# Projection and turn of the next heads behind the first value product in every attention group, four feed-forward tiles in TensorE's loop, and the order of SyncE's pad writes

## The reference, cut to what matters

```
kv   = concatenate([xn @ Wkv.T, ln @ Wlkv.T])          # 64 context rows and 1024 normed token rows
q    = ln @ Wq.T
attn = softmax(rmsnorm(q) * SCALE @ rmsnorm(k).T + mask)
x    = x + tanh(g_xattn) * ((attn @ v) @ Wo.T + bo)
probs = softmax(layernorm(x) @ w_router); top 2 of 8 experts per token
x    = x + tanh(g_ffn) * sum over the 2 experts of weight * (gelu(y @ w1 + b1) @ w2 + b2)
```

## Time and profile before

| | |
|---|---|
| median of 3 runs | 915.76 us |
| the profiled execution: own time | 922.48 us |
| its span | 920.7 us |
| TensorE matmuls, busy | 856.9 us, 93% of the span |
| VectorE busy | 647.2 us, 70% |
| ScalarE busy | 514.5 us, 56% |
| GpSimd busy | 331.9 us, 36% |
| mean granted TensorE clock | 0.989 of full speed |

### The profile page before, as it was taken

The page is one execution under the profiler, slowest core; times in us unless marked ns, Lnnn a source line. Parts: engine busy times, 40 slices in busy tenths (PEclk is TensorE's granted clock), DMA queues, the critical chain, the costliest instruction groups (busy, mean ns, idle before and its releaser), DMA issues.

```text
span 920.7 us, 19517 instructions
## 1 busy us (share of the span) xinstructions
PE 856.9 (93%) x5968; PEld 656.6 (71%) x5968; DVE 647.2 (70%) x1500; ACT 514.5 (56%) x1371; POOL 331.9 (36%) x241
## 2 busy tenths in 40 slices
PE   3898899998999989999999998999999999999995
PEld 3644455554455544554459998999999999999995
DVE  5767667677776767667697788775756776676695
ACT  2668676687757878558762654443433443353462
POOL 2332323323285322653134328532322223232233
PEclk9899999999999999999999999999999999999998
DMA  4801000120012201120034449452342525253272
GB/s 126 243 1 49 1 1 1 47 94 1 1 51 88 93 1 47 41 92 18 1 104 122 118 102 255 103 142 46 85 94 46 133 48 139 46 137 49 37 229 24
DMA packets 71899, 70.32 MB, mean 76 GB/s; under 512 B 18592, under 2 KB 66976, under 8 KB 71840
## 3 DMA queue, kind: packets, MB, share of 16 engines
q1 hardware_dynamic: 57696, 52.73, 19.5%
q0 software_dynamic: 13152, 16.86, 10.5%
q10 hardware_dynamic: 992, 0.00, 0.1%
HBM read 44.04 MB, written 26.31 MB: 76 GB/s over the span
## 4 chain that ended last, share of the span: by engine, by line
PE 47%; issue 15%; DVE 15%; POOL 10%; DMA 5%; ACT 5%; SPq 2%; another core or an unknown queue 1%; DVEq 0%; POOLq 0%; ACTq 0%
PE psS L1685 17%; PE psF L1881 8%; PE psO L1881 8%; POOL rr L676 6%; PE psO L1818 4%; DMA lnf<-routed 4%; PE psS L1802 4%; POOL routed L686 4%; DVE p_sum L1136 3%; PE psF L1685 2%; PE psF L1849 1%; ACT sq L823 1%; DMA xr<-in_x 1%; ACT p_ring L867 1%; DVE qkd L1110 1%
## 5 line engine op out<-in xcount | busy, mean ns | idle before, releaser
L884 ACT ACTIVATE V<-psS,b_col 128x256 f32<-128x256 f32 x280 | 117.0, 470 | 212.2 <-PE psS L1685 193.3
L694 POOL DMA_INDIRECT out<-V,token_i x70 | 122.5, 1749 | 262.6 <-DVE V L1327 241.7
L676 POOL TENSOR_TENSOR rr<-ssm,minus_half 128x4 f32<-128x4 f32 (+1 forms) x72 | 119.0, 1652 | 255.1 <-DVE ssm L1100 254.9
L867 ACT ACTIVATE p_ring<-psS,shift 128x1024 f32<-128x1024 f32 x128 | 136.5, 1111 | 70.4 <-PE psS L1802 70.2
L1818 PE MATMUL psO<-p_ring,V 128*64 128x512 f32 x576 | 149.2, 615 | 0.0
L1136 DVE TENSOR_TENSOR p_sum<-p_sum,p_ring 128x1024 f32<-128x1024 f32 (+1 forms) x112 | 136.1, 1215 | 0.8
L1881 PE MATMUL psF<-ln_hi,K 128*128 128x256 f32 x560 | 123.7, 284 | 0.3 <-DVE K L1306 0.3
L1802 PE MATMUL psS<-Q,K 64*128 64x512 f32 x864 | 121.4, 413 | 0.2 <-ACT p_ring L867 0.2
L1802 PEld LDWEIGHTS psS<-Q,K 64*128 64x128 f32 x864 | 77.2, 187 | 61.4 <-issue 43.5
L1881 PE MATMUL psO<-ln_hi,K 128*128 128x256 f32 x560 | 120.5, 279 | 0.0
L1306 DVE TENSOR_TENSOR K<-V,K 128x512 fp32r<-128x512 f32 x140 | 97.1, 693 | 4.8
(11 more groups left out here) (289 smaller groups left out, 1761.1 us busy)
## 6 DMA issues: line engine op xcount, KB each, us to landing
xr<-in_L_ffn_w SPq DMA_DIRECT2D x11, 1024.0 KB, 8.3
xn<-in_L_ffn_w SPq DMA_DIRECT2D x11, 1024.0 KB, 5.4
lnf<-routed SPq DMA_DIRECT2D x35, 258.0 KB
routed<-pad_rows SPq DMA_DIRECT2D x17, 258.0 KB, 9.5
xr<-in_x SPq DMA_DIRECT2D x8, 512.0 KB, 4.5
xb<-in_x SPq DMA_DIRECT2D x4, 1024.0 KB, 5.9
out<-xb SPq DMA_DIRECT2D x4, 1024.0 KB, 4.7
b_raw<-in_L_ffn_b SPq DMA_DIRECT2D x11, 128.0 KB, 3.1
```

The source lines that it names most:

```text
L676: pool.tensor_tensor(rr[0:p, c % 2, n], ssm[0:p, c % 2, n], minus_half[0:p, n], ALU.pow).then_inc(rr_ready, 1)
L694: pool.indirect_dma_start(out_rows, bass.IndirectOffsetOnAxis(ap=token_i[:, m:m + 1], axis=0), y_out[:, m, :], None, bounds_check=NTOK - 1 ...
L867: act.activation(p_ring[0:p, u % RING, :], psS[u % 2][0:p].rearrange("p a n -> p (a n)"), ACT.Exp, bias=bias).then_inc(exp_done, 1)
L884: act.activation(g32[:, q % 2, (c % 2) * TM:(c % 2 + 1) * TM], psH[q][:, (c % 2) * TM:(c % 2 + 1) * TM], ACT.Gelu_apprx_tanh, bias=b1_col[ ...
```

## The change

Four edits. (1) In the attention `tile_steps` stands behind the first value product in all groups. (2) In the last window the ranks of the sequence before move from the late uses of group 5 to behind the scores of group 6, ahead of the sums. (3) On TensorE tiles 5 to 8 of the feed-forward part go into the loop. (4) SyncE writes five of the eight pads before `load_rows(7)` and three behind it.

```diff
@@ mid_uses and late_uses
+                if w + 1 == WINDOWS and i == 6:
+                    return [("ranks", b - 1)]
...
-                    if i == (5 if last else 6):
+                    if i == 6 and not last:
                         return [("ranks", b - 1)]
@@ SyncE
-                for e in range(NE):
+                for e in range(5):
                     pad(e)
                 load_rows(7, kept_row(7))
+                for e in range(5, NE):
+                    pad(e)
                 load_w1(3)
@@ TensorE, the loop over the groups
                     for u in (2 * g, 2 * g + 1):
                         scores(u)
                     if w + 1 == WINDOWS and i == 6:
+                        ranks(b - 1)
                         sums(2 * g - 4)
-                    if i != 5:
-                        tile_steps(g)
                     if g >= 1 and not folded:
                         values(2 * g - 2)
-                    if i == 5:
-                        tile_steps(g)
+                    tile_steps(g)
                     for name in mid_uses(w, i):
-                        use(name)
+                        if name[0] != "ranks":
+                            use(name)
@@ TensorE, the feed-forward part
-                for t in range(5, KTILES):
-                    first_layer(t)
-                    turn_tile(t + 1)
-                    second_layer(t)
-                with pe.Fori(KTILES, SURE - 1) as t:
+                with pe.Fori(5, SURE - 1) as t:
                     first_layer(t)
                     turn_tile(t + 1)
                     second_layer(t)
```

More of the change, by code:

```diff
@@ L1907, in _ @@
                     w, i = divmod(g, GROUPS)
+                    b = w // 2
                     folded = w + 1 == WINDOWS and i == 5
```

## The result

The changed kernel takes **930.88 us**, the median of 4 runs (925.84 to 933.29), against 915.89 for the kernel before beside it: ratio **1.0149 (95% interval 1.0123 to 1.0174)**, 15 us slower. The forecast was 919.9 with a range up to 923.5: the direction is right, the size is not. In a second comparison (experiment 12) the two kernels stood at 931.96 and 921.27, ratio 1.0113 (1.0098 to 1.0128); so the effect is 10 to 15 us.

What follows compares the result with a forecast made beforehand. TensorE works 407 of 437 us in the attention, with a round trip in force in plain groups. Terms 2.61 + 0.68 - 0.1 + 0.68 - 2.1 + 2.0 + 0.3 = +4.1 on 915.76 gave 919.9 us, range 914.5 to 923.5.

Steps and rivals of the forecast that it cites:

- The chain: Attention round trip from projection through ssm, rr and qkd to the turn: everything behind ssm comes 0.68 us later.
- The circle: Plain attention groups: either order leaves the same 3.46 us of TensorE work between projection and next turn.
- The rival in which the turns' waits go: Attention: nearly all 21 turn waits for qkd vanish, 10.9 us, 13.0 with the bank waits, giving 902.8; chance 0.2.
- group 3: Windows 1, 3 and 5: later ssm delays heads_lo and the turn of normed rows, +0.87 us each, 2.61 together.
- group 2 of even windows: Windows 2, 4 and 6: the projection's 0.67 us wait for its bank goes, -0.7 us each, -2.1 together.
- their groups 4 to 8: Windows 2, 4 and 6: the chain from ssm delays the turn of rows, +0.68 us each, +2.0 together.
- groups 4 to 0: Windows 3 and 5, VectorE never free up to the output projection: +0.68 us in window 3, -0.1 in window 5.
- TensorE's clock drops once more: Group 3 of windows 3 and 5, waits of 2.18 us: clock falls, 1.5 us each, 922.9 us; chance 0.14.
- the stall moves: Feed-forward: tile 7's turn wait of 2.98 us shifts to its second layer; 0 taken, bounds -3.0 and +0.3.
- the row-based 0: TensorE's loop, tiles 5 to 8: rows show 11.80 us a tile written out, 11.64 in the loop, so no effect.
- The rival in which tile 7's stall is really won: Feed-forward: 3.0 us gained at tile 7, the rest as forecast, 916.9 us, no change; chance 0.13.
- The signs written down beforehand: Profile marks listed in advance across attention and tile 7, such as ssm at 5.2 us behind the scores in all groups.

Runs made afterwards that it cites:

- experiment 12: The changed kernel once more with no edit, against the kernel before on another chip: 931.96 us against 921.27, ratio 1.0113.
- Experiment 5: Kernel before, with projection and turn behind the first value product also in group 2 of windows 2, 4 and 6: 919.63 us against 923.37, ratio 0.9967.
- experiment 6: Kernel before with tile_steps behind the first value product everywhere except groups 2 and 4 of odd windows: 927.03 us, ratio 1.0040.
- Experiment 11: Kernel before with tile_steps behind the first value product everywhere, and VectorE's second addition ahead of mean squares in group 0 of windows 1, 3, 5: 933.81 us, 1.0141.
- Experiment 1: Kernel before with only tile_steps moved behind the first value product in all groups: 928.41 us, ratio 1.0109.
- experiment 8: Kernel before with tile_steps behind the first value product everywhere, and VectorE's second addition behind scale_heads: 956.49 us, ratio 1.0361.
- experiment 2: Changed kernel with the old order back in the attention, leaving ranks, pads and loop: 915.85 us, ratio 0.9972 to the kernel before.
- experiment 3: Kernel before with only the pads split, five before load_rows(7) and three behind: 917.38 us, ratio 0.9998.
- experiment 4: Kernel before with only tiles 5 to 8 put into TensorE's loop: 916.36 us, ratio 0.9982.
- experiment 7: Kernel before with tile_steps behind the first value product everywhere, and the second ahead of the norm's turn in group 3 of windows 1, 3, 5: 930.11 us, 1.0083.
- experiment 9: Kernel before with ranks, pads and loop edits, and the new order in group 2 of windows 2, 4, 6: 918.07 us against 921.27, ratio 0.9960.
- experiment 10: Ranks, pads, loop, new order in group 2 of windows 2, 4, 6, second value product ahead of norm's turn; against kernel before: 917.47 us, 0.9958.

## Why the prediction was right in direction and wrong in size

**The chain** held. `ssm` is 0.68 later, and the period of a plain group with a binding round trip is unchanged at 5.33 us, as forecast. **The circle** held in this but not in its sum: the work between projection and next turn was put at 3.46 us in both orders. The rows give 4.25 - 0.71 = 3.54 before and, from 130.37 to 134.28 less the wait of 0.24, 3.67 after. A value product that stands apart costs some 0.15 more, which shortens the wait where the round trip binds and lengthens the groups where nothing waits (4.87 to 5.03 in group 4 of the even windows). The rival in which the turns' waits go (chance 0.2), at 902.8 us, is what the total of 13.3 against 8.1 us alone would have suggested, and the kernel is slower by 10 us or more with 5.2 us less of that wait.

**The three terms with the most behind them** (group 3, group 2 of even windows, their groups 4 to 8) were +2.5 together in the forecast and measure +3.2. Experiment 5 shows the gain and experiment 6 the loss by itself.

**The step that failed, first part: the list of VectorE's customers was incomplete.** The forecast followed the shift of 0.68 only to `heads_lo`, in front of the turn of normed rows and the output projection. VectorE's second addition stands behind `mean_squares` in every group, so it shifts too, and in group 0 of windows 1, 3 and 5 the sums wait for it: +2.2 us, priced nowhere. Experiment 11 takes that wait away. The "groups 4 to 0" of the forecast end with the output projection, in group 0 of an even window; group 0 of an odd one stands in no term.

**Second part: a delay was taken to be paid once per stretch.** "It sees the projection of group 4 another 0.68 later" was right, but in window 3 the sums of group 5 wait 0.94 instead of 0.28 for that (245.56), which lengthens the group by 0.65. TensorE starts the next groups in step with VectorE again, and there each projection is 0.68 behind the old order once more; the output projection of window 4's group 0 waits 0.96 and adds 0.87. Between the two only 0.2 was given back, so +1.3 instead of +0.7. Experiment 6 shows that these are two payments: with the old order back in group 4 the one at the sums is gone and the one at the output projection stays. In window 5 the first value product does hide the shift at the output projection (0.16 of wait, +0.07), but not at the sums of group 5, so +0.5 instead of -0.1. For each place where TensorE waits for VectorE and is thereby brought back into step, the shift has to be paid anew.

**Third part: the clock.** The rival "TensorE's clock drops once more" (chance 0.14) happened. It named the places, group 3 of windows 3 and 5, with waits of 2.18, and a price of 1.5 us each; measured are 2.33, and 1.56. With a wait of 2.33 us there (the changed kernel twice, experiments 1 and 11) the clock falls behind it in window 3 in four profiles out of four, in window 5 in three of four; in experiment 8, where the wait is 2.56, in both, 1.3 us after it. With a wait of 1.3 us there (the kernel before and experiments 2 to 7 and 9, eight profiles) it falls in none. I had held against it the 2.98 of tile 7, and that one wait without a drop outweighed the one with it. That the longer wait brings the drop is shown by experiments 6 and 7, which shorten it to 1.3 in two ways and have no drop; why it doesn't always is open. The rule of the Trainium skill that the prediction cited (TensorE: Matmul & The Clock Gate, section on oscillation) points the right way, but a gap alone doesn't decide: in window 1, behind a wait of 3.25 us the clock fell in one profile of those four, behind 2.2 us in two of eight.

**The small edits.** Pads: "the stall moves" is right; 0 measured (-0.0002), 0 forecast. But the stall of 2.98 that it was reckoned from is one of that profile: 0.91 in experiment 4, with the same pads. Loop: no stall from the branch; the row-based 0 held, and if anything it is -1.6 us. The Trainium skill's rule that a taken branch outside the fetched window stalls the engine (Runtime: NRT & Kernel Launch, section on instruction fetch) finds nothing here: the step from tile 6 to tile 7 takes 11.64 us in the loop and written out (experiments 2 and 3). No run shows whether the branch leaves that window. Ranks: -0.2, forecast 0. The rival in which tile 7's stall is really won (chance 0.13) is not what the pads do. The three edits together gained 2.6 us, where 0 was forecast with bounds that held it.

**The sum.** Attention without drops +8.2 instead of +4.1 (+8.9 without the start, which is not the edit's), and drops +2.1, 10.3 altogether. Experiment 1 measures 10.0 us for edit 1 alone (ratio 1.0109), so this part is accounted for. Less the 2.6 us of the small edits the whole change should be 7.7 us slower; measured are 10.7 in the second comparison and 15 in the first. The remaining 3 and 7 us are open. The feed-forward part may take them, as it did in experiments 9 and 10, or drops that come and go: the second profile of the changed kernel has one of double length and a single one more than the first, and its attention is 4.4 us longer. The runs of the first comparison have mean clocks from 0.980 to 0.987, by and large lower the slower they are (925.84 us at 0.987, 928.97 at 0.985, 932.78 at 0.980, 933.29 at 0.982); a drop of 3.4 us at half speed takes 0.0018 off the mean. The median run lies 5 us above the profiled one; two further drops would be 3 of them. That is argued and not shown, since those runs left no profile. The range ended at 923.5: it took in the two drops, but neither of the first two parts.

**The signs written down beforehand.** Right: the turn of group 6 without a wait, the bank wait of group 2 in the even windows gone, `ssm` 5.26 behind the scores, tile 7's turn without a wait, and nearly so the turn of normed rows (2.3 us of wait and 3.25 in window 1, forecast 2.1 to 2.2 and 3.1). Missed: windows 3 and 5 were to be longer by 1.6 and 0.8 and are 2.2 and 2.3 longer without their drops; the even ones were to be the same and are 1.1, 1.1 and 0.3 longer.

## What to carry to other kernels

When work is moved behind something on one engine, list every instruction behind its consumer on the other engines, and every later place that waits for one of them; each wait that brings the two engines back into step charges the shift again. If the consumer's engine has no slack, a move that shortens the most visible wait can be a loss, and the move pays only at the few places where it removes a wait of another kind (here a bank, -0.7 us each). Read a wait that grows past what the clock has borne in that place as two costs, the wait itself and a possible spell at half clock.

## What was not expected of the hardware

GpSimd's root of a 128x4 tile takes 1.01 us alone and 1.92 beside VectorE's addition of two 128x1024 tiles. The Trainium skill (GPSIMD Engine Reference, section on specifications) has the two share their SBUF interfaces, with contention where a VectorE instruction has two inputs in SBUF, as this addition does; the rows agree, and 0.9 us is its price here.

The order of the same matmuls has a price: a plain group of scores, turn, projection and two value products, without any wait, lasts 4.87 us with the products adjacent and 5.03 with turn and projection between them. Why is not shown.

TensorE's clock falls to 1.2 GHz for about 3.4 us at a time, costing 1.0 to 1.6 us each, at places that are nearly fixed in some groups and change from run to run in others. Two kernels (experiments 6 and 7) ran the whole attention with none in their profiles.
